# Layer-norm arithmetic moved from GpSimd to VectorE in a convolution-attention-recurrence kernel, with extra TensorE products in the last part

## The chip, the cores and the metric

One core of a Trainium2 chip runs the whole program. The metric is the device time of that core in microseconds (us), the median of several executions. TensorE (PE, with PEld for its weight loads), VectorE (DVE), ScalarE (ACT), GpSimd (POOL) and the DMA queue of SyncE (SP) each run their own list of instructions in order and wait for one another through semaphores.

## The reference, cut to what matters

The input x is 4 batches of 64 channels and 1024 positions (tokens).

```python
x = x + wo @ (softmax(k^T q) v)             # "conv": per batch, 1024 x 1024 scores, no scale
t = to_tokens(x)
t = t + causal_attention(ln(t))             # 8 heads of 64, then @ Wo    (ln: layer norm 1)
t = t + ffn(ln(t))                          # (ln: "norm 3")
# ffn: Wx = ln(t) @ W^T, batch norm over all tokens, then
#      y[t] = sigmoid(Wx[t] + y[t-1] @ V^T) over 1024 steps
```

Both layer norms take each token's mean and variance over 64 channels. The recurrence is solved by sweeps over all positions at once and the last step's change is tested against a limit.

## The kernel before

The main part is a loop over 352 **items** in numbered **slots**. An item is one 128 x 512 tile of scores: TensorE makes it in a bank (L511 conv, L537 attention), ScalarE takes exp of it twice (L775 into `probs`, f32; L779 into `probs_high`, f16), GpSimd subtracts the two into `probs_low` (`pool_low`, L1250), and TensorE multiplies high and low parts by the values (L574, L576, L578) six slots later. Every fourth item of conv and every sixth of attention is "whole": it is used in f32 (L570) and has no work for GpSimd. Slots 0 to 63 are conv, a unit of 16 for each batch. From slot 64 a **unit** is a pair of heads of one batch: 18 slots, in nine **pairs** of slots; at each even slot two items are made, and four units make a batch.

Two units ahead of their use, TensorE makes the raw scores of a later unit (L483, L497) in two banks and VectorE takes their row maxima (L903, two for each pair; L897 in conv). The same two banks serve each pair, so TensorE can't write the masks (L483) of a pair before VectorE has read the pair before it. The partial maxima of a unit are joined by two instructions at L909, once a unit, which makes them a mark for the length of a unit. VectorE also scales finished outputs (L979, L983), makes the low parts of values, queries and keys (L959, L964, L968), and GpSimd adds the scaled outputs to the tokens (`pool_add`, L1260).

**Norm 1** has statistics and application. VectorE takes the statistics of each 128-token tile (L1004, L1007), adds epsilon (L1013) and makes a first guess of the reciprocal root (L988), for three groups: batch 0, batch 1, batches 2 and 3 together (`LN1_GROUPS`), at slots 22, 75 and 129 (`LN1_START_SLOT`). GpSimd refines the guess with three Newton steps of four instructions (`pool_newton`, L1271 to L1274), and in `pool_ln1` subtracts the mean (L1286), multiplies (L1288), sets channel 0 to one (L1290) and copies the result beside itself (L1291) into `xh`; this happens at slots 23, 80, 136 and 214, one for each batch. TensorE transposes `xh` at the key slots (L651), ScalarE and VectorE make the high and low keys.

**Norm 3** of batches 0 and 1 (start at slot 237) and of batch 2 (slot 309) goes the same way: VectorE's guess, GpSimd's twelve Newton instructions four slots later, GpSimd's application (`pool_ln3`, L1295, L1296) from 8 slots later. The last batch's norm is done by VectorE with `dve_newton` (L994 to L996, three instructions a step, each linked: the next one starts when a semaphore tells that the one before has finished).

The order on each engine is the order of the program in each slot. On VectorE it is: scaling, maxima, low parts, and last `dve_norms(g)`. So what a norm does at slot g stands behind the maxima of g and ahead of all of the next slot.

**The last part**: TensorE transposes the last norm's output (L584), multiplies by W (L702, L711), VectorE takes the batch statistics (L1144 to L1169), and sweeps follow: TensorE L730, L731 (then L738 to L747), ScalarE L861, L870, L875.

## Time and profile before

| | us |
|---|---|
| median of 3 runs | 570.09 (568.32 to 572.07) |
| the profiled execution: its own time | 568.85 |
| its span, first to last instruction | 567.0 |
| busy: PE / PEld | 490.0 / 323.0 |
| busy: DVE | 398.8 |
| busy: ACT | 429.3 |
| busy: POOL | 424.4 |
| chain that ended last, by engine | PE 45%, DVE 22%, POOL 17%, ACT 9%, issue 6% |

The profiled execution's time is 1.9 us above its span, and 1.2 us below the median. The mean clock that TensorE was granted is 0.974 of full speed. Busy time of PE counts matmuls to their modelled ends, so that a busy PE is not a PE at its peak.

### The profile page before, as it was taken

Reading aid. Unit: us, or ns where it says so; the run is one execution under the profiler, and the core shown is the slowest. Engines: PE = TensorE matmul, PEld = TensorE weight load, DVE = VectorE, ACT = ScalarE, POOL = GpSimd, SP = SyncE. Lnnn points to the kernel's source line nnn. Section 1 sums busy time; section 2 is a strip of 40 time slices with the busy share of each in tenths; the row PEclk is TensorE's granted clock in tenths of the full one; section 3 lists DMA queues with packets and bytes.
Section 4 is the critical chain, followed back from the end, with each engine's and each line's share of the span. In section 5 each row is a group of like instructions: output and inputs, shape, how many; then the busy total and the mean of one; then the engine's idle time right before and its main releaser. Section 6 shows DMA issues by size and latency. Waiting matters only on the chain.

```text
span 567.0 us, 16744 instructions
## 1 busy us (share of the span) xinstructions
PE 490.0 (86%) x6771; PEld 323.0 (57%) x6771; DVE 398.8 (70%) x909; ACT 429.3 (76%) x832; POOL 424.4 (75%) x463
## 2 busy tenths in 40 slices
PE   4699978988799998889999988998999999787783
PEld 1277655655565755565666756565666766564431
DVE  5878888767678786576767676766767786328757
ACT  3488867866778878587888878787888878785593
POOL 3867965857988797968788797899788799985002
PEclk9999999989999999799999999999999999998698
DMA  9100000000000000000000000000000000000001
GB/s 230 68 3 2 2 20 1 4 1 3 1 22 2 3 3 2 3 1 21 2 3 2 4 3 1 21 3 1 1 3 3 2 3 2 2 2 2 0 2 74
DMA packets 3580, 7.46 MB, mean 13 GB/s; under 512 B 1168, under 2 KB 1456, under 8 KB 3376
## 3 DMA queue, kind: packets, MB, share of 16 engines
q1 hardware_dynamic: 3056, 5.34, 3.5%
q8 instruction: 54, 0.88, 0.7%
q10 hardware_dynamic: 448, 1.05, 0.6%
q14 instruction: 22, 0.18, 0.1%
HBM read 4.22 MB, written 1.05 MB: 9 GB/s over the span
## 4 chain that ended last, share of the span: by engine, by line
PE 45%; DVE 22%; POOL 17%; ACT 9%; issue 6%; DMA 1%; DVEq 0%; SPq 0%; POOLq 0%; ACTq 0%
POOL probs_low L1250 10%; PE bank L537 9%; DVE attn_partial_max L903 7%; ACT probs_high L779 6%; PE bank L497 6%; PE bank L570 5%; PE bank L574 4%; DVE conv_partial_max L897 3%; PE bank L578 3%; PE bank L576 3%; PE bank L455 2%; PE bank L522 2%; PE bank L483 2%; PE bank L456 2%; POOL tokens L1260 2%
## 5 line engine op out<-in xcount | busy, mean ns | idle before, releaser
L1250 POOL TENSOR_TENSOR probs_low<-probs,probs_high 128x512 f16<-128x512 f32 x288 | 327.6, 1158 | 77.5 <-ACT probs_high L779 76.7
L775 ACT ACTIVATE probs<-bank 128x512 f32<-128x512 f32 x352 | 214.7, 611 | 84.2 <-PE bank L537 69.0
L903 DVE TENSOR_REDUCE attn_partial_max<-bank 128x1 f32<-128x512 f32 (+2 forms) x288 | 185.3, 685 | 99.5 <-PE bank L497 99.0
L779 ACT ACTIVATE probs_high<-bank 128x512 f16<-128x512 f32 x288 | 176.8, 614 | 0.0
L574 PEld LDWEIGHTS bank<-values_high,probs_high 128*128 128x128 f16 x1152 | 105.7, 98 | 74.2 <-issue 35.8
L574 PE MATMUL bank<-values_high,probs_high 128*128 128x65 f16 x1152 | 128.8, 196 | 15.5 <-POOL probs_low L1250 11.4
L576 PE MATMUL bank<-values_low,probs_high 128*128 128x64 f16 x1152 | 127.6, 194 | 0.0
L578 PE MATMUL bank<-values_high,probs_low 128*128 128x65 f16 x1152 | 127.1, 194 | 0.0
L576 PEld LDWEIGHTS bank<-values_low,probs_high 128*128 128x128 f16 x1152 | 106.9, 99 | 3.2
L578 PEld LDWEIGHTS bank<-values_high,probs_low 128*128 128x128 f16 x1152 | 107.2, 98 | 0.0
L570 PE MATMUL bank<-values,probs 128*128 128x65 f32 x512 | 71.7, 278 | 0.8 <-POOL probs_low L1250 0.8
L570 PEld LDWEIGHTS bank<-values,probs 128*128 128x128 f32 x512 | 64.7, 192 | 3.5 <-POOL probs_low L1250 1.0
L497 PE MATMUL bank<-attn_keys_high,queries_high 64*128 64x512 f16 (+3 forms) x384 | 56.7, 332 | 7.9 <-ACT probs_high L779 6.0
L1260 POOL TENSOR_TENSOR tokens<-scaled_outputs,tokens 128x256 f32<-128x256 f32 x71 | 51.7, 729 | 8.0 <-DVE scaled_outputs L983 3.3
L537 PE MATMUL bank<-queries_high,attn_keys_high 64*128 64x512 f16 (+3 forms) x384 | 55.6, 326 | 1.1 <-ACT probs_high L779 1.1
L537 PE MATMUL bank<-queries_high,attn_keys_low 64*128 64x512 f16 (+3 forms) x384 | 55.5, 325 | 0.0
L537 PE MATMUL bank<-queries_low,attn_keys_high 64*128 64x512 f16 (+3 forms) x384 | 55.5, 325 | 0.0
L897 DVE TENSOR_REDUCE conv_partial_max<-bank 128x1 f32<-128x512 f32 x64 | 42.8, 687 | 5.8 <-PE bank L470 4.7
L983 DVE TENSOR_TENSOR scaled_outputs<-bank,reciprocal_denominators 128x256 f32<-128x256 f32 x72 | 30.6, 425 | 7.6 <-DVE reciprocal_denominators L979 0.5
L522 PE MATMUL bank<-causal_masks,identity_bf 128*128 128x128 bf16 x256 | 27.5, 219 | 6.6 <-ACT probs_high L779 6.4
L497 PEld LDWEIGHTS bank<-attn_keys_high,queries_high 64*128 64x128 f16 x384 | 15.3, 93 | 29.7 <-issue 6.8
L1343 POOL TENSOR_TENSOR x_split<-probs 128x512 f32<-128x512 f32 x4 | 4.2, 1092 | 36.1 <-ACT probs L878 36.1
(192 smaller groups left out, 708.9 us busy)
## 6 DMA issues: line engine op xcount, KB each, us to landing
x_channels<-in_x_cm SPq DMA_DIRECT2D x6, 256.0 KB, 7.6
tokens<-in_x_tm SPq DMA_DIRECT2D x1, 1024.0 KB, 10.4
out<-ln_channels SPq DMA_DIRECT2D x4, 256.0 KB, 2.0
attn_weights<-in_attn_w ACTq DMA_DIRECT2D x1, 512.0 KB, 6.2
attn_keys_split<-attn_keys_high SPq DMA_DIRECT2D x4, 128.0 KB, 2.3
attn_keys_split<-attn_keys_low SPq DMA_DIRECT2D x4, 128.0 KB, 2.4
queries_high<-minus_max_rows SPq DMA_DIRECT2D x32, 2.0 KB
x_channels<-in_x_cm ACTq DMA_DIRECT2D x2, 128.0 KB, 3.2
```

Source lines behind the costliest of these rows:

```text
L497: last[r] = nc.tensor.matmul(prep_bank(m + r)[:, at * P:(at + tiles) * P], q[rows(r), t * P:(t + 1) * P], xs_hi[rows(r), b * N + j0 * P:b ...
L537: last[r] = nc.tensor.matmul(ST[(i + r) % ST_RING][:, at * P:(at + tiles) * P], keys[rows(r), b * N + j * P:b * N + (j + 1) * P], queries[ ...
L570: ins = nc.tensor.matmul(dst, e32[:, item % E_RING, cols], v32[v % 2][:, j, r, :], start=opens, stop=True, skip_group_check=True)
L574: nc.tensor.matmul(dst, hi, v_hi[v % 2][:, j, r, :], start=opens, stop=False, skip_group_check=True)
L576: nc.tensor.matmul(dst[:, 0:C], hi, v_lo[v % 2][:, j, r, :], start=False, stop=False, skip_group_check=True)
L578: ins = nc.tensor.matmul(dst, lo, v_hi[v % 2][:, j, r, :], start=False, stop=True, skip_group_check=True)
L775: ins = nc.scalar.activation(e32[:, i % E_RING, :], o[:], ACT.Exp, scale=scale)
L779: ins = nc.scalar.activation(p_hi[:, i % P_RING, :], o[:], ACT.Exp, scale=scale)
L897: nc.vector.reduce_max(cmx[v % 2][:, t, part:part + 1], o[:], AX).then_inc(s_prep_used, 1)
L903: nc.vector.reduce_max(dst, o[:].rearrange("p (n w) -> p n w", n=n), AX).then_inc(s_prep_used, 1)
L1250: nc.gpsimd.tensor_tensor(out=p_lo[:, i % P_RING, :], in0=e32[:, i % E_RING, :], in1=p_hi[:, i % P_RING, :], op=ALU.subtract).then_inc(s_r ...
L1260: nc.gpsimd.tensor_tensor(out=dst, in0=scaled[:, half % S_RING, :, :], in1=dst, op=ALU.add).then_inc(s_added, 1)
```

## The change

1. **Norm 1's Newton steps and application go to VectorE.** `pool_newton` and `pool_ln1` are gone. `dve_ln1_start` links its guess, and the three slots behind it hold one Newton step each (three linked instructions). `dve_ln1_apply(b, part)` makes two tiles: one `tensor_scalar` for each tile subtracts the mean and multiplies, with its input broadcast over both copies. Four parts make a batch: at slots 26, 27, 28, 29 for batch 0, and at 82, 138 and 212, each with three more at steps of two slots. The last part ends with a linked memset of channel 0.
2. **Norm 3's Newton steps** go to VectorE as well, one for each of the slots 238 to 240 and 310 to 312. GpSimd keeps the application.
3. Key slots of batch 1 move from 88, 92 to 92, 96.
4. **`pe_keep_clock(bank, n)`** puts n products of 128 x 256 bf16 (identity by masks), whose result nobody reads, at five places of the last part: 8, 6, 22, 3 and 18.

```diff
-LN1_APPLY_SLOT = (23, 80, 136, 214)
-KEY_SLOTS = ((32, 34), (88, 92), (154, 160), (226, 232))
+LN1_APPLY_SLOT = (26, 82, 138, 212)
+LN1_APPLY_PACE = (1, 2, 2, 2)
+KEY_SLOTS = ((32, 34), (92, 96), (154, 160), (226, 232))
...
+        def pe_keep_clock(bank, n):
+
+            for _ in range(n):
+                nc.tensor.matmul(bank[:, 0:2 * P], identbf[:], masks[:].rearrange("p a c -> p (a c)"),
+                                 start=True, stop=True)
...
             pe.wait_ge(s_l3t, 2)
+            pe_keep_clock(MX[0], 8)
             pe.wait_ge(s_l3, 3)
             pe_transposes(MX[1], xh3, 2).then_inc(s_tr, 1)
+            pe_keep_clock(MX[0], 6)
             pe.wait_ge(s_trc, 1)
             nc.tensor.matmul(ST[0][:], ffn_w[:, 0, :], xh3T[:, 2 * CW:3 * CW], start=True, stop=True).then_inc(s_wxp, 1)
+            pe_keep_clock(MX[0], 22)
             for t in range(TPC):
                 pe.wait_ge(s_l3, 4 + t)
                 ins = pe_transpose(LN_BANKS[t // 2], xh3, 3, t)
                 if t % 2:
                     ins.then_inc(s_tr, 1)
             pe.wait_ge(s_aux_used, len(AUXES))
+            pe_keep_clock(ST[1], 3)
             for h in range(2):
                 pe.wait_ge(s_trc, h + 2)
...
             pe.wait_ge(s_bn3, 1)
             pe.wait_ge(s_t2c, 2)
+            pe_keep_clock(MX[0], 18)
...
-            rsqrt_start(rstd1[:, cols], var1[:, cols]).then_inc(s_rstd1, 1)
+            dve_rsqrt_start(rstd1[:, cols], var1[:, cols])
+
+        def dve_ln1_apply(b, part):
+
+            if b and part == 0:
+                nc.vector.wait_ge(s_aux, AUX_OF["keys", 2 * b - 1] + 1)
+            for t in (2 * part, 2 * part + 1):
+                n = b * NT + t
+                ins = nc.vector.tensor_scalar(xh[:, t, :, :],
+                                              tok[:, (t * B + b) * C:(t * B + b + 1) * C].unsqueeze(1)
+                                              .to_broadcast([P, 2, C]),
+                                              mv1[:, n, 0:1], rstd1[:, n:n + 1], ALU.subtract, ALU.mult)
+            if part == NT // 2 - 1:
+                link(ins)
+                nc.vector.memset(xh[:, :, :, 0:1], 1.0).then_inc(s_xt, 1)
...
+                if 0 < g - LN1_START_SLOT[group] <= 3:
+                    cols = slice(b0 * NT, b1 * NT)
+                    dve_newton(rstd1[:, cols], var1[:, cols], nwt1[:, cols])
+            for b in range(B):
+                part, odd = divmod(g - LN1_APPLY_SLOT[b], LN1_APPLY_PACE[b])
+                if 0 <= part < NT // 2 and not odd:
+                    dve_ln1_apply(b, part)
...
             for slot, b0, b1 in ((LN3_PAIR_SLOT, 0, 2), (LN3_THIRD_SLOT, 2, 3)):
-                if g == slot:
-                    v, r, _ = ln3_views(b0, b1, 0, NT)
-                    link(nc.vector.tensor_scalar_add(v, mv4[:, :, b0:b1, 1], LN_EPS))
-                    rsqrt_start(r, v).then_inc(s_rstd3, 1)
+                if 0 <= g - slot <= 3:
+                    ln3_rstd(g - slot, b0, b1, ready=s_rstd3)
...
-                for b in range(B):
-                    if g == LN1_APPLY_SLOT[b]:
-                        pool_ln1(b)
                 for n, slot in enumerate((LN3_PAIR_SLOT, LN3_THIRD_SLOT)):
-                    if g == slot + 4:
+                    if g == slot + 8:
                         pool.wait_ge(s_rstd3, n + 1)
-                        v, r, w = ln3_views(2 * n, 2 + n, 0, NT)
-                        pool_newton(r, v, w)
-                    if g == slot + 8:
                         pool.wait_ge(s_added, (B + (2 + n) * H) * NC)
```

## Rows read from the trace of the kernel before

**Rows 1.** Windows, one unit each from L909 to L909: busy us, clock, DMA.

```profile
131.31:158.44 27.13, 23.00 (x347) 15.59 (x348) 18.04 (x36) 20.16 (x40) 23.07 (x34) 1.00 0.01 2
207.56:236.11 28.55, 24.20 (x341) 16.01 (x342) 17.11 (x35) 19.35 (x38) 24.10 (x35) 0.88 0.01 2
236.11:263.34 27.23, 24.46 (x376) 16.71 (x374) 20.23 (x52) 22.11 (x43) 20.56 (x21) 1.00 0.05 12
287.03:310.72 23.69, 22.54 (x358) 15.43 (x354) 16.50 (x33) 19.85 (x40) 19.82 (x20) 1.00 0.01 2
334.42:362.99 28.57, 24.26 (x366) 16.37 (x362) 20.23 (x52) 21.75 (x42) 22.75 (x23) 1.00 0.05 11
387.88:414.64 26.76, 25.16 (x390) 17.38 (x386) 17.82 (x37) 21.69 (x43) 22.88 (x23) 1.00 0.01 2
438.33:462.38 24.05, 22.70 (x358) 15.45 (x353) 19.03 (x49) 19.91 (x40) 19.89 (x20) 1.00 0.01 2
```

**Rows 2.** Waits, stretch 296.6 to 320.3, a unit that no norm touches.

```profile
DVE attn_partial_max L903 <- PE bank L497: 7.1, 8, 2.0
```

**Rows 3.** Timeline of POOL, 218 to 231: start, us, instruction, idle before.

```profile
220.53 0.23 POOL L1271 TENSOR_TENSOR newton_scratch<-ln_rstd,ln_var_eps 128x16 f32<-128x16 f32 x1
...
223.85 0.22 POOL L1274 TENSOR_TENSOR ln_rstd<-newton_scratch,ln_rstd 128x16 f32<-128x16 f32 x1
224.15 1.05 POOL L1286 TENSOR_TENSOR ln_out<-tokens,ln_mean_var 128x512 f32<-128x512 f32 x1
...
227.12 2.27 POOL L1250 TENSOR_TENSOR probs_low<-probs,probs_high 128x512 f16<-128x512 f32 x2
```

**Rows 4.** Waits of PE, stretch 217 to 246.7.

```profile
PE bank L574 <- POOL probs_low L1250: 3.4, 2, 3.1
```

**Rows 5.** Timeline of POOL and of DVE, 510 to 520.

```profile
511.37 6.73 POOL L1250 TENSOR_TENSOR probs_low<-probs,probs_high 128x512 f16<-128x512 f32 x6
...
513.71 1.08 DVE L988 TENSOR_SCALAR ln_rstd<-ln_var_eps 128x4 int32<-128x4 int32 x1
514.82 1.08 DVE L994 TENSOR_TENSOR ln_newton_scratch<-ln_rstd,ln_var_eps 128x4 f32<-128x4 f32 x1
515.93 1.08 DVE L995 SCALAR_TENSOR_TENSOR ln_newton_scratch<-ln_newton_scratch,ln_rstd 128x4 f32<-128x4 f32 x1
...
518.16 0.17 DVE L994 TENSOR_TENSOR ln_newton_scratch<-ln_rstd,ln_var_eps 128x4 f32<-128x4 f32 x1
```

**Rows 6.** Timeline of DVE, PE and POOL around slots 130 to 134.

```profile
208.46 1.27 DVE L903 TENSOR_REDUCE attn_partial_max<-bank 128x1 f32<-128x512 f32 x2
209.88 0.38 PE L483 MATMUL bank<-causal_masks,identity_bf 128*128 128x128 bf16 x4
210.11 2.27 POOL L1250 TENSOR_TENSOR probs_low<-probs,probs_high 128x512 f16<-128x512 f32 x2 [0.49 <-ACT probs_high L779]
210.74 1.29 DVE L903 TENSOR_REDUCE attn_partial_max<-bank 128x4 f32<-128x512 f32 x2 [0.56 <-PE bank L497]
212.54 2.27 POOL L1250 TENSOR_TENSOR probs_low<-probs,probs_high 128x512 f16<-128x512 f32 x2 [0.16 <-ACT probs_high L779]
213.02 0.39 PE L483 MATMUL bank<-causal_masks,identity_bf 128*128 128x128 bf16 x4
```

**Rows 7.** Timeline of DVE, 525.4 to 527.

```profile
525.45 0.98 DVE L1135 TENSOR_SCALAR ln_tokens<-tokens,ln_mean_var,ln_rstd 128x64 f32<-128x64 f32 x4
```

**Rows 8.** Window 52 to 64, in conv, columns as in rows 1.

```profile
52.00:64.00 12.00, 10.78 (x135) 8.08 (x132) 10.45 (x35) 9.72 (x21) 10.17 (x22) 1.00 0.02 4
```

**Rows 9.** Windows in the last part, columns as in rows 1.

```profile
520.50:530.80 10.30, 7.75 (x22) 4.52 (x23) 7.53 (x37) 2.56 (x5) 0.72 (x1) 0.50 0.00 1
534.20:537.60 3.40, 3.14 (x8) 0.82 (x9) 2.60 (x7) 3.40 (x8) 0.00 (x0) 0.50 0.00 0
```

**Rows 10.** Timeline of PE and ACT, the last part.

```profile
522.08 2.07 PE L702 MATMUL bank<-ln_channels,ffn_weights 128*128 128x512 f32 x2 [0.69 <-ACT ln_channels L845]
525.82 1.14 PE L584 MATMUL bank<-constants,ln_tokens 128*128 128x128 f32 x4 [1.67 <-DVE ln_tokens L1135]
527.08 2.04 PE L711 MATMUL bank<-ln_channels,ffn_weights 128*128 128x256 f32 x4
534.46 0.59 PE L730 MATMUL bank<-wx_fp,identity_fp 128*128 128x512 f16 x1 [2.34 <-ACT y_fp L861]
536.53 3.06 ACT L870 ACTIVATE y_fp<-bank 128x512 f16<-128x512 f32 x6
...
555.19 3.60 PE L752 MATMUL bank<-probs,ffn_weights 128*128 128x512 f32 x8
```

26 lines of the change are left out of this document (1 added, 25 removed).

## The prediction, made before the changed kernel was run

> **What bounds the kernel now.** I read the page first: no engine is saturated (PE 490 us busy of 567, POOL 424, DVE 399) and the chain that ended last changes between PE, DVE, POOL and ACT. So I read the windows unit by unit [rows 1]. A unit of attention that no norm touches lasts 23.69 us; in it POOL is busy for 19.8, DVE for 16.5, and the maxima on DVE wait for TensorE for 7.1 us, some 0.8 us for each of nine pairs [rows 2]. The loop runs at the pace of its dependences, and an engine with idle time still has only a small cushion at each place. Units with norm work are longer: 28.55, 28.57, 27.13 and 26.76 us. The clearest case is batch 2's norm: POOL spends 220.53 to 227.12, 6.6 us, on Newton steps and application [rows 3], TensorE waits 3.4 us for `probs_low` behind it [rows 4], and the unit's mean granted clock is 0.88.
>
> DVE's cushion is uneven. Around slot 130 the masks for the next maxima start at 209.88, 0.15 us after DVE finished its maxima (208.46 + 1.27): TensorE was waiting for DVE. A pair later DVE has 0.56 us idle, and TensorE comes 0.99 us after it (210.74 + 1.29 to 213.02) [rows 6]. So VectorE can take 0.56 + 0.99 = 1.55 us more between slots 130 and 132; beyond that TensorE is late, and behind it scores, exp and everything else.
>
> **What leaves POOL.** I take from each long unit what POOL's block explains, against 23.69 [rows 1].
> - Batch 2: 28.55 − 23.69 = 4.9 us. Rows 4 and the lowered clock fit. The bound above is POOL's whole 6.6.
> - Batch 3 (slot 214, application only): 28.57 − 23.69 = 4.9, but the unit 236 to 263 has the same key work and statistics, no norm on POOL, and 27.23, that is 3.5 over. That leaves 1.3; I take 1.4 for rounding against what falls before the mark.
> - Batch 1: 27.13 − 23.69 = 3.4, with part of the keys' cost in it. I take 2.6.
> - Norm 3 of batches 0 and 1: 26.76 − 23.69 = 3.1, most of it transposes and products by W on TensorE, which stay. I take 0.6. The third batch: the unit up to its start has 24.05, 0.4 over; I take 0.5.
> - Batch 0 in conv: 0.6, little, as units there have other limits.
>
> Together 10.6 us. Below, this could be 6 (only what rows 4 show, and a little of the others), above some 15.
>
> **What comes to DVE, Newton steps.** What does a small DVE instruction cost while POOL works? While POOL runs six `probs_low` back to back from 511.37 (6.73 us), each linked instruction of DVE on four columns takes 1.08 us, and 0.17 us at 518.16, after POOL has ended [rows 5]. It waits out one POOL instruction each time. This holds for `tensor_scalar` (L988), `tensor_tensor` (L994) and `scalar_tensor_tensor` (L995). The Trainium skill states the same as a rule (SBUF — State Buffer, "Who interferes with whom"): a DVE instruction with two SBUF inputs, or in a two-port mode, is blocked until a GpSimd instruction that started first has ended. The trace agrees, with 1.08 against 0.17 us. It is a rule that speaks against this change: it makes of 12 instructions of 0.2 us on POOL nine that may take 1.1 us on DVE.
>
> Two of three steps, at slots 130 and 131, fall between two maxima. Six instructions: 6 × 0.2 = 1.2 us if POOL never holds them, 6 × 1.1 = 6.6 if always. By rows 6, POOL pauses before 210.11 and before 212.54. I lay them in: two pass by 210.1, the third ends at 211.3, the fourth at 212.4, the fifth in the pause, the sixth at 213.7. So about 3.9 us from 209.75, and 3.9 − 1.55 = 2.35, say 2.3 us of delay for TensorE. The third step, behind the maxima of 132, meets a POOL that has run dry, since the scores are late: 0.6 us, in the idle time. Slots 76 to 78, 238 to 240 and 310 to 312 have the same place in their units or nearly so. 4 × 2.3 = 9.2 us (bounds: 0, when 1.2 stays under the cushion, and 4 × 5.0 = 20).
>
> **Application.** Four of today's on 64 columns take 0.98 us [rows 7], so a part of two, of 128 columns each, some 0.55 us unhindered. Each reads and writes SBUF as L988 does, which waits in rows 5; I expect the same here, though its broadcast input is not shown anywhere. Both of a part held: 0.55 + 2 × 1.1 = 2.7 us. When DVE sets the pace, POOL has often finished when a part begins, so I take one wait of some 0.65: 1.2 us a part. Against the cushion of 0.8 each part delays by 0.4: 12 parts give 4.9 us for batches 1 to 3 (bounds 0 and 23). The memset is 0.1 and hidden.
>
> **Batch 0.** Conv from 52 to 64: DVE is busy 10.45 of 12.0 us [rows 8], so 1.55 is free; POOL is busy 10.17, of which some 6 are this norm and go away. Newton 9 × 0.45 = 4.0, four parts × 0.7 = 2.8, minus 1.55, and as much again because four banks, not two, let TensorE run ahead: 3.7, I take 3.5 (bounds 0.5 and 9).
>
> **The last part.** The granted clock is 0.50 (1.2 GHz) from 520.5 to 530.8 and from 534.2 to 537.6, after stretches in which TensorE mostly waited [rows 9]. On the path that sets the end stand L584 (1.14 us) and L711 (2.04 for four pieces of 256 columns); L752's eight pieces of 512 columns at full clock take 3.60, some 0.43 each and so 0.22 for 256 [rows 10]. At 2.4 GHz L711 is bound by its two copies and takes about 1.1, a gain of 0.95; L584 gives 0.3 of 1.14, as its tiles come from DVE one by one; the small product before the batch statistics gives 0.2. The first sweep was slow too, but L870 runs back to back from 536.53 (six in 3.06 us), so ScalarE sets the pace and only 0.1 is won. That is 1.55; I take 1.5. The added products: half of a 512-column product of 0.22 is 0.11 us each at full clock. 22 × 0.11 = 2.4 us behind L702 ends before L584's start at 525.82, if L702 is done by 523; the 18 fit in the 2.3 us idle ahead of L730.
> In the Trainium skill (TensorE: Matmul & The Clock Gate, "What's actually happening") activity releases the throttle. The trace agrees as far as it goes: the clock of 0.50 follows TensorE's idle stretches.
>
> Moving the keys of batch 1 by four slots costs nothing: batch 1's first queries are made at slot 104, and between lie only one unit's rows of maxima in SP's queue.
>
> **Sum.** 9.2 + 4.9 + 3.5 − 10.6 − 1.5 = +5.5 us. The profiled execution, 568.85, becomes 574.4; on the median, 570.09, it is 575.6. I say 574.8.
>
> **Rivals.**
> - *The ports rarely meet (faster).* With POOL rid of the 6.6 us blocks, DVE's instructions fall into its pauses: Newton 2.8 us between the maxima, 1.25 us over the cushion four times = 5.0, parts of 0.8 or less = 0, batch 0 1.5. 6.5 − 10.6 − 1.5 = −5.6: 563 us; with Newton's delay gone too, 5.0 less, 558. For it: POOL's pauses in rows 6. Against it: POOL is busy 84% of an untouched unit. It decides in favour of faster when six instructions take under 2.8 us. 27%.
> - *Parts wait twice (slower).* After each `tensor_scalar` POOL's waiting instruction goes first, and the second waits again: 2.3 us a part instead of 1.2, 12 × 1.1 = +13: 588 us. For it: the chain in rows 5 alternates in just that way. Against it: the two of a part aren't linked. 18%.
> - *The products are in the way.* If the clock stays at 0.50 through the 22, they take 22 × 0.21 = 4.7 us, from 524.2 to 528.9, and L584 is 3.1 us late instead of early: +4.6, 579 us. 8%.
> - My forecast: 45%; 2% left for others.
>
> Range 561 to 586: from the faster rival's neighbourhood to just under the doubled parts. The forecast's own range is 569 to 581. About 1% (5.7 us) is what a measurement of this kernel can tell from no change. Faster by over 1% (below 564.4): most of the first rival, 24%. Slower by over 1% (above 575.8): nearly half of the forecast's own spread and the two slower rivals, 38%. Same 38%.
>
> **What would show it.** In the changed trace, L994 to L996 at slots 130, 131 at 1.1 us each and the masks L483 some 2 us later than their place; if instead they take 0.17, the first rival. The unit 207.56 to 236.11 falls from 28.55 to about 28.0 (−4.9, +2.3, +1.6 and +0.4). The parts' `tensor_scalar` at 0.3 against 1.2 us and more tells the second rival. A POOL row of 6.6 us between two `probs_low` must be gone. In the last part the granted clock must be near 1.00 between 523 and 538 and L711 near 1.1 us; if it is 0.50 with 22 products ahead of L584, the third. I am wrong altogether if DVE's delays don't reach TensorE, that is if idle time on DVE before L903 stays as it was and units are still shorter.

## The result, and the profile after

| | before | after |
|---|---|---|
| median | 570.31 (568.32 to 572.07, 4 runs) | 581.82 (581.04 to 583.14, 4 runs) |
| ratio | | 1.0205, 95% interval 1.0165 to 1.0245 |
| profiled execution: own time, span | 568.85, 567.0 | 581.04, 579.2 |
| mean granted clock | 0.974 | 0.977 |
| busy: PE / DVE / ACT / POOL | 490.0 / 398.8 / 429.3 / 424.4 | 495.3 / 436.1 / 429.4 / 401.4 |
| chain that ended last | PE 45%, DVE 22%, POOL 17% | PE 43%, DVE 35%, POOL 6% |

The change made the kernel slower by 11.5 us, 2%. In a second comparison (experiment 9) the same kernel had 582.19 to 586.56 us in four executions; two more, of 591.37 and 602.92 us, ran in a slower state with a lower granted clock and are left out. Over the eight that are left the median is 582.75, and the profiled one is the fastest of them.

POOL lost 23.0 us of busy time and DVE gained 37.3. In the chain DVE rose by 13 points and POOL fell by 11. The main wait of each of the two engines tells the same (kernel after; us in total, times, longest):

```profile
POOL probs_low L1278 <- ACT probs_high L791: 116.1, 119, 4.6
DVE attn_partial_max L915 <- PE bank L504: 77.8, 87, 2.0
```

POOL now waits 116 us for ScalarE (76.7 before), DVE 78 us for TensorE (99.0 before): the cushion moved from DVE to POOL. Each kernel has its own line numbers; in the changed one L490 is the mask product, L504 the scores for maxima, L787 the first exp, L915 the maxima, L1003 to L1005 the Newton step, L1031 the application, L1278 `probs_low`.

Windows as in [rows 1], kernel after, from L921 to L921: the units of batch 1's and batch 2's norm, an untouched one, and that of norm 3's pair.

```profile
135.28:163.57 28.29, 22.76 (x343) 15.36 (x344) 26.04 (x54) 19.75 (x39) 20.22 (x20) 1.00 0.01 2
213.67:242.81 29.14, 23.16 (x353) 15.63 (x353) 26.22 (x54) 20.06 (x39) 20.85 (x22) 1.00 0.01 2
293.43:317.12 23.69, 22.54 (x358) 15.43 (x353) 16.52 (x33) 19.84 (x40) 19.81 (x20) 1.00 0.01 2
371.09:400.44 29.35, 26.20 (x345) 16.88 (x346) 21.12 (x44) 20.26 (x41) 21.70 (x22) 0.88 0.01 2
```

The untouched unit is again 23.69 us. Batch 2's unit, 28.55 before, is 29.14 though its clock rose from 0.88 to 1.00; norm 3's pair of batches, 26.76 before, is 29.35 and its clock fell to 0.88. In the units of norm 1 DVE is now busy for 26 us of 28 or 29.

**The ledger.** A mean over a unit hides which edit cost what. The kernel has 352 items, and each begins with one exp of a full bank on ScalarE (L787, L775 before). I took the 352 start times of both traces and compared the distance from each even slot to the next: a delay "at slot 130" is what the changed kernel needs more from the exp of item 130 to that of item 132. Outside the slots below the two kernels agree to 0.07 us, mostly to 0.02, so most differences can be put to one edit. A "fall" is a stretch in which the granted clock is 0.50 (1.2 GHz) and not 1.00 (2.4 GHz).

| part | forecast | measured, slots |
|---|---|---|
| batch 0 on DVE | +3.5 | +5.8 (24 to 31) |
| Newton, batch 1 | +2.3 | +1.4 (76, 78) |
| Newton, batches 2 and 3 | +2.3 | +1.5 (130, 132) |
| Newton, norm 3 of the pair | +2.3 | +4.5 (240, 242) |
| Newton, norm 3 of the third | +2.3 | +3.5 (312) |
| application of batches 1 / 2 / 3 | 1.6 each | +1.4 / +3.75 / +2.5 (90; 140, 144, 146; 216 to 220) |
| key slots of batch 1 | 0 | +1.0 (94, 96) |
| POOL relieved of batch 1 / 2 / 3 | −2.6 / −4.9 / −1.4 | −1.7 / −4.9 / −0.8 (86, 88; 142; 222) |
| POOL relieved of norm 3, and of batch 0 | −1.1, −0.6 | −2.5 (254, 302, 324, 326), 0 |
| a fall of the clock that before had at 121.2 | 0 | −1.4 (68, 74) |
| start | 0 | −0.4 |
| last part | −1.5 | −1.4 |
| sum | +5.5 | +12.2 |

The spans give the same, 579.2 − 567.0 = 12.2. Where two edits act on the same slots, the ledger has only their sum. Slots 86, 88 and 142 hold the relief of POOL together with parts of the application, which experiment 7 takes apart. And batch 1's keys left slots 88 and 92 for 92 and 96, so some of what slots 86 and 88 gained may be what 94 and 96 lost: no run moves the keys alone. POOL's block of 6.6 us [rows 3] was worth 4.9, as forecast; what took its place on DVE cost more.

**The Newton steps, as predicted, and what is queued behind them.** Timeline of DVE, kernel after, slots 130 to 131, and then of POOL:

```profile
214.68 1.29 DVE L915 TENSOR_REDUCE attn_partial_max<-bank 128x1 f32<-128x512 f32 x2
215.88 0.17 DVE L1003 TENSOR_TENSOR newton_scratch<-ln_rstd,ln_var_eps 128x16 f32<-128x16 f32 x1
216.08 0.17 DVE L1004 SCALAR_TENSOR_TENSOR newton_scratch<-newton_scratch,ln_rstd 128x16 f32<-128x16 f32 x1
216.29 1.11 DVE L1005 SCALAR_TENSOR_TENSOR ln_rstd<-newton_scratch,ln_rstd 128x16 f32<-128x16 f32 x1
217.44 1.08 DVE L1003 TENSOR_TENSOR newton_scratch<-ln_rstd,ln_var_eps 128x16 f32<-128x16 f32 x1
218.56 0.17 DVE L1004 SCALAR_TENSOR_TENSOR newton_scratch<-newton_scratch,ln_rstd 128x16 f32<-128x16 f32 x1
218.76 0.17 DVE L1005 SCALAR_TENSOR_TENSOR ln_rstd<-newton_scratch,ln_rstd 128x16 f32<-128x16 f32 x1
218.97 0.28 DVE L939 TENSOR_SCALAR minus_max_rows<-bank 16x128 f16<-16x128 f32 x1
219.18 1.26 DVE L915 TENSOR_REDUCE attn_partial_max<-bank 128x4 f32<-128x512 f32 x2
```

```profile
216.22 2.27 POOL L1278 TENSOR_TENSOR probs_low<-probs,probs_high 128x512 f16<-128x512 f32 x2 [0.49 <-ACT probs_high L791]
218.78 2.29 POOL L1278 TENSOR_TENSOR probs_low<-probs,probs_high 128x512 f16<-128x512 f32 x2 [0.29 <-ACT probs_high L791]
```

Two instructions pass in POOL's pause at 0.17 us, two wait out one `probs_low` each, and the last two pass again: 3.05 us for six. `minus_max_rows` (L939) and the maxima of the next pair begin only behind them; TensorE waits 0.34 us for the one and 0.66 us for the other.

Norm 3's pair has the same order of work, but it meets POOL otherwise (DVE, then PE; the two instructions before these lines, from 373.11, take 0.34 and 0.17 us):

```profile
373.70 1.14 DVE L1005 SCALAR_TENSOR_TENSOR ln_rstd<-ln_newton_scratch,ln_rstd 128x16 f32<-128x16 f32 x1
374.87 1.08 DVE L1003 TENSOR_TENSOR ln_newton_scratch<-ln_rstd,ln_var_eps 128x16 f32<-128x16 f32 x1
375.98 0.18 DVE L1004 SCALAR_TENSOR_TENSOR ln_newton_scratch<-ln_newton_scratch,ln_rstd 128x16 f32<-128x16 f32 x1
376.19 1.06 DVE L1005 SCALAR_TENSOR_TENSOR ln_rstd<-ln_newton_scratch,ln_rstd 128x16 f32<-128x16 f32 x1
377.29 0.28 DVE L939 TENSOR_SCALAR minus_max_rows<-bank 16x128 f16<-16x128 f32 x1
```

```profile
377.63 0.23 PE L462 MATMUL bank<-value_matrix_high,attn_keys_split 128*128 128x128 f16 x1 [1.37 <-DVE minus_max_rows L939]
...
378.91 0.59 PE L490 MATMUL bank<-causal_masks,identity_bf 128*128 128x128 bf16 x4 [0.63 <-DVE attn_partial_max L915]
```

Here three instructions are held, six take 4.2 us (373.11 to 377.25), and TensorE waits twice: 1.37 us for `minus_max_rows` (L939), which is queued behind the Newton steps here too, and 0.63 us for the maxima. The granted clock then falls to 0.50 at 378.08.

**The application.** All 32 instructions (duration ns, minimum, median and maximum), kernel after:

```profile
L1031 DVE TENSOR_SCALAR ln_out<-tokens,ln_mean_var,ln_rstd x32: 332/398/1237, 61.5 to 344.2; 128x128 f32<-128x128 f32 x32
```

0.33 us when it passes, up to 1.24 when held. The 24 of batches 1 to 3 take 17.3 us together: 14 of them are over 0.5 us, and in three of the twelve parts both are.

### The profile page after: what moved, and what is told of

It is laid out like the page before. It is cut to its first block, busy times and chain, and to the rows that moved or that the text cites. A ratio compares the mean times of both kernels' runs of the same rounds, so it can differ in the third digit from the quotient of the medians.

```text
span 579.2 us, 16871 instructions
## 1 busy us (share of the span) xinstructions
PE 495.3 (86%) x6828; PEld 327.3 (57%) x6828; DVE 436.1 (75%) x990; ACT 429.4 (74%) x832; POOL 401.4 (69%) x387
## 3 DMA queue, kind: packets, MB, share of 16 engines
q10 hardware_dynamic: 448, 1.05, 0.6%
HBM read 4.22 MB, written 1.05 MB: 9 GB/s over the span
## 4 chain that ended last, share of the span: by engine, by line
PE 43%; DVE 35%; ACT 9%; POOL 6%; issue 5%; DMA 1%; DVEq 0%; SPq 0%; POOLq 0%; ACTq 0%
DVE attn_partial_max L915 11%; PE bank L544 9%; ACT probs_high L791 6%; PE bank L504 6%; POOL probs_low L1278 5%; PE bank L577 4%; DVE conv_partial_max L909 4%; PE bank L581 4%; DVE ln_out L1031 3%; PE bank L585 2%; PE bank L529 2%; PE bank L583 2%; PE bank L462 2%; PE bank L490 2%; PE bank L463 2%
## 5 line engine op out<-in xcount | busy, mean ns | idle before, releaser
L1278 POOL TENSOR_TENSOR probs_low<-probs,probs_high 128x512 f16<-128x512 f32 x288 | 328.2, 1157 | 117.0 <-ACT probs_high L791 116.1
L787 ACT ACTIVATE probs<-bank 128x512 f32<-128x512 f32 x352 | 214.9, 612 | 99.8 <-PE bank L544 80.0
L915 DVE TENSOR_REDUCE attn_partial_max<-bank 128x1 f32<-128x512 f32 (+2 forms) x288 | 185.2, 685 | 78.5 <-PE bank L504 77.8
L504 PE MATMUL bank<-attn_keys_high,queries_high 64*128 64x512 f16 (+3 forms) x384 | 56.9, 333 | 9.5 <-ACT probs_high L791 5.9
L909 DVE TENSOR_REDUCE conv_partial_max<-bank 128x1 f32<-128x512 f32 x64 | 42.9, 687 | 5.5 <-PE bank L477 4.7
L490 PE MATMUL bank<-causal_masks,identity_bf 128*128 128x128 bf16 x256 | 27.6, 221 | 8.7 <-DVE attn_partial_max L915 7.7
L529 PE MATMUL bank<-causal_masks,identity_bf 128*128 128x128 bf16 x256 | 28.1, 223 | 6.1 <-ACT probs_high L791 6.0
L504 PEld LDWEIGHTS bank<-attn_keys_high,queries_high 64*128 64x128 f16 x384 | 15.5, 93 | 31.3 <-DVE attn_partial_max L915 10.8
```

The source lines that it names most:

```text
L504: last[r] = nc.tensor.matmul(prep_bank(m + r)[:, at * P:(at + tiles) * P], q[rows(r), t * P:(t + 1) * P], xs_hi[rows(r), b * N + j0 * P:b ...
L787: ins = nc.scalar.activation(e32[:, i % E_RING, :], o[:], ACT.Exp, scale=scale)
L909: nc.vector.reduce_max(cmx[v % 2][:, t, part:part + 1], o[:], AX).then_inc(s_prep_used, 1)
L915: nc.vector.reduce_max(dst, o[:].rearrange("p (n w) -> p n w", n=n), AX).then_inc(s_prep_used, 1)
L1278: nc.gpsimd.tensor_tensor(out=p_lo[:, i % P_RING, :], in0=e32[:, i % E_RING, :], in1=p_hi[:, i % P_RING, :], op=ALU.subtract).then_inc(s_r ...
```

## The experiments

All were compared with the kernel before in runs of the same chip. Experiments 3 to 6 and 12 ran on one chip, 1, 2, 7 and 8 on a second, 9 to 11 on a third, so variants of different groups are compared by their ratios to the kernel before. Where the profiled execution of a variant is read slot by slot, it is by the ledger as above.

**1. The last part alone.** The kernel before with the five groups of products, nothing else:

```diff
+            pe_keep_clock(MX[0], 8)      # and 6, 22, 3, 18 at the same places as in the changed kernel
```

> The kernel before with only the added products of the last part. Both theories of the last part: from the last item's exp to the end the changed trace is 1.4 us shorter. Theory (the products alone did it): 568.9 against 570.3 of the kernel before, and 1.4 us less of span behind the last item. Rival (the last part is shorter as GpSimd or VectorE comes to it in another state): no change, 570.3.

Measured: 568.60 us (566.89 to 571.40, 10 runs) against 569.47 (30 runs): ratio 0.9992, interval 0.9965 to 1.0019. Not to be told from no change, and the interval reaches down to 2 us of gain. The trace shows why it is so little. PE, this variant:

```profile
522.46 1.13 PE L710 MATMUL bank<-ln_channels,ffn_weights 128*128 128x512 f32 x2
533.97 0.38 PE L741 MATMUL bank<-wx_fp,identity_fp 128*128 128x512 f16 x1 [0.42 <-ACT y_fp L872]
554.82 3.93 PE L763 MATMUL bank<-probs,ffn_weights 128*128 128x512 f32 x8
```

The product by W takes 1.13 us, not 2.07 [rows 10], and the first sweep starts 1.3 us sooner behind the last item (17.14 us after item 352 at 516.83; before 534.46 − 516.02 = 18.44). In the changed kernel and in every variant with the products that distance is the same to 0.03 us. But the products stop there, and the clock falls later: from 552.1 in this trace, and the eight f32 products behind the sweeps take 3.93 us instead of 3.60. Part of the gain is given back 20 us behind the edit. The loop is unedited here, and still its trace differs from that of the kernel before by −1.4 us at slots 68 to 74, where the kernel before had a fall of the clock, and by +1.6 us at slots 36 to 40, where this one has it (74.2). So the −1.4 us at slots 68 and 74 in the ledger isn't the change's doing.

**2. Norm 1 back on POOL.** The products and norm 3's Newton steps on DVE stay:

```diff
-LN1_APPLY_SLOT = (26, 82, 138, 212)      # parts on DVE
+LN1_APPLY_SLOT = (23, 80, 136, 214)      # pool_newton and pool_ln1, as before
-KEY_SLOTS = ((32, 34), (92, 96), ...
+KEY_SLOTS = ((32, 34), (88, 92), ...
```

> The changed kernel with all of norm 1 back on GpSimd as before (old slots too); norm 3's Newton steps stay on VectorE and the added products stay. Theory: what is left of the change is +3.4 and +2.0 us by norm 3 and -1.4 by the products, so 570.3 + 4.1 = 574.4. If the two norms' parts add up, this and the run with norm 3 back on GpSimd together explain the whole: 581.8 - 574.4 = 7.4 us for norm 1. Rival (the parts overlap, one hides the other's delay): above 577 or below 572.

Measured: 573.37 us (571.33 to 576.56), ratio 1.0055 (1.0028 to 1.0081), against an expectation of 574.4. So most of the loss belongs to norm 1. Slots 240 and 312 have +3.6 each, with the clock at 0.50 in both, and slots 254 and 302 to 326 have the 2.5 us of POOL's relief: nearly what the changed kernel has there.

**3. Norm 3's Newton steps back on POOL.** Norm 1 stays on DVE:

```diff
-                if 0 <= g - slot <= 3:
-                    ln3_rstd(g - slot, b0, b1, ready=s_rstd3)
+                if g == slot:
+                    ...                                        # guess on DVE
+                    if g == slot + 4:
+                        pool.wait_ge(s_rstd3, n + 1)
+                        ...
+                        pool_newton(r, v, w)
```

> The changed kernel with norm 3's Newton steps back on GpSimd, all else as changed. Theory (port): comparing item starts of the two traces, these steps cost VectorE 4.5 us at slots 242 to 244 and 3.5 us at slot 314, while taking them from GpSimd gave back 1.1 and 1.4 us. So 5.5 us less than the changed kernel: 576.3 against 581.8. Rival (the whole loss is norm 1's, as that is most of what moved): at most 1 us less, 581.

Measured: 580.74 us (578.75 to 581.05), ratio 1.0173 (1.0147 to 1.0200). The time that I expected was missed by 4.4 us, and the intervals of this ratio and of the changed kernel's, 1.0205 (1.0165 to 1.0245), overlap. Yet by slots the edit did what it should: 4.5 us less at 240 and 242, 3.5 less at 312, 1.1 and 1.2 more at 254 and 324 where POOL's blocks are back, 5.6 us net. It was lost elsewhere: +1.6 at slots 90 and 92, +1.4 at 218, 0.6 at 26 to 30, 1.4 in the last part, all places whose code is unchanged, and 0.7 at the start: both spans are 579.2. Windows of two slots from 218 (us, busy by engine, granted clock, DMA), first the changed kernel and then this variant:

```profile
339.88:344.64 4.76, 2.89 (x47) 2.05 (x48) 4.46 (x13) 1.57 (x3) 3.38 (x4) 1.00 0.00 0
```

```profile
342.71:349.17 6.46, 4.78 (x47) 3.22 (x47) 6.02 (x17) 1.58 (x4) 3.40 (x4) 0.60 0.01 3
```

The same 47 matmuls and the same delay before them, but a clock of 0.60 and 1.7 us more (1.4 with the slot behind it). What decides over such a fall was open here; run 9 below takes it up.

**4. Newton steps one to a pair of slots**, so that two never fall between the same maxima:

```diff
-                if 0 < g - LN1_START_SLOT[group] <= 3:
+                wide = (1, 2, 3) if group == 0 else (1, 3, 5)
+                if g - LN1_START_SLOT[group] in wide:
...
-                if 0 <= g - slot <= 3:
-                    ln3_rstd(g - slot, b0, b1, ready=s_rstd3)
+                if g - slot in (0, 1, 3, 5):
+                    ln3_rstd((g - slot + 1) // 2, b0, b1, ready=s_rstd3)
```

> The changed kernel with one Newton step for each pair of slots (behind slots start+1, +3, +5) for the groups in attention, instead of three in a row of slots. Same instructions, same number. Theory (port waits against a small cushion of VectorE between two maxima): three instructions take at most 3.3 us, and mostly 1 to 2.4, against cushions of 1.55, 2.76 and 1.07 us. The four groups' 10.8 us of delay become 3 to 4, so 574 to 575 against 581.8. Rival (VectorE's work in sum is what counts, wherever it stands): no change, 581 to 582.

Measured: 580.60 us (579.82 to 580.77), ratio 1.0179 (1.0158 to 1.0200). By slots the Newton steps of the four groups cost 2.2, 0.8, 0.65 and 1.4 us, 5.0 in all instead of 10.8, so 5.8 of the some 7 us expected were won there. Falls of the clock at 127.1, 164.7 and 246.6, which the changed kernel's trace has not, and a longer last part take 5.1 us of it, and slots 24 to 30, with a longer fall than there, 0.9 us more. A lone step can still cost: at 381.28 two of three instructions are held for 1.0 us each.

**5. Two of three Newton steps with an operand in a bank.** Variance and scratch of the attention groups lie in PSUM, so that no instruction of the step reads two tiles of SBUF:

```diff
+            v, w = in_psum(b0, b1)               # AUX[:, 384:...], AUX[:, 416:...]
+            dve_newton(r, v, w, s_newt if step == 2 else None)
...
+                if g in (78, 132, 240, 312):
+                    pe.wait_ge(s_newt, (78, 132, 240, 312).index(g) + 1)
```

> The changed kernel with variance and scratch of the first two Newton steps of each attention group in a PSUM bank that is free there, so that each instruction reads only one operand from SBUF. Same places, same number of instructions plus one small copy a group; TensorE waits for the second step before it uses the bank again. Theory (the wait is for the SBUF port that VectorE and GpSimd share): each of the six instructions takes 0.2 us with GpSimd busy too, 1.2 us in sum, under the cushion of 1.55; 10.8 us of delay at these groups become 0 to 1.5, so 571 to 572.5 against 581.8. Rival (a linked instruction is slow while GpSimd works for another reason, such as the semaphore): they stay at 1.1 us, 581 to 582.

Measured: 582.38 us (577.50 to 582.99), ratio 1.0191 (1.0139 to 1.0242); 571 to 572.5 was expected. DVE and POOL, at norm 3's pair:

```profile
378.76 0.17 DVE L1008 SCALAR_TENSOR_TENSOR ln_rstd<-bank,ln_rstd 128x16 f32<-128x16 f32 x1
378.97 0.18 DVE L1006 TENSOR_TENSOR bank<-ln_rstd,bank 128x16 f32<-128x16 f32 x1
379.19 0.18 DVE L1007 SCALAR_TENSOR_TENSOR bank<-bank,ln_rstd 128x16 f32<-128x16 f32 x1
379.40 0.17 DVE L1008 SCALAR_TENSOR_TENSOR ln_rstd<-bank,ln_rstd 128x16 f32<-128x16 f32 x1
```

```profile
378.85 2.27 POOL L1308 TENSOR_TENSOR probs_low<-probs,probs_high 128x512 f16<-128x512 f32 x2 [0.22 <-ACT probs_high L794]
```

The mechanism stands: three instructions begin while POOL works and take 0.17 to 0.18 us, and six take 1.2 us instead of 4.2. My edit brought a wait of its own, though. The bank is TensorE's for small products, so TensorE has to wait until the steps have left it:

```profile
379.63 0.28 PE L622 MATMUL bank<-constants,row_max 128*16 128x128 f32 x1 [1.14 <-DVE ln_rstd L1008]
```

The groups cost 1.6, 1.5, 1.1 and 1.3 us, one slot pair earlier than before, 5.5 in all. That would be 5.3 us less than in the changed kernel's trace. And again falls that this trace has not, at 27.5, 164.1 and 345.0, and one more in the last part took the gain.

**6. Products in the stall.** Forty small products ahead of the masks of slots 242 and 314:

```diff
+                if g in (242, 314):
+                    for _ in range(40):
+                        nc.tensor.matmul(OT[1][:, 384:512], identbf[:], masks[:, 0, :], ...)
```

> The changed kernel with 40 products of 128 columns, read by nobody, in TensorE's list ahead of the masks of slots 242 and 314, where it waits for VectorE for some 3 us anyway. Theory (part of the delay there is the clock: it fell to 0.50 at 378.1 for 6.8 us and at 480.5 for 3.4 us): the clock stays at full speed, slot 242 and 244 lose 2.6 instead of 4.5 us and slot 314 2.6 to 2.9 instead of 3.5. In sum 2 to 2.8 us less, 579 to 580 against 581.8. Rival (the clock's fall costs nothing, since the waits are VectorE's): 581 to 583, with 40 x 0.056 = 2.2 us of products in the stall.

Measured: 587.99 us (582.61 to 591.58), ratio 1.0263 (1.0205 to 1.0322): slower than both expectations. PE, this variant:

```profile
383.19 2.40 PE L698 MATMUL bank<-causal_masks,identity_bf 128*128 128x128 bf16 x40
```

The trace has no fall of the clock at slots 240 or 312. But TensorE's longer wait there is the one for `minus_max_rows`, ahead of these products, so they start only behind it and take 2.40 us where 0.63 us were idle: slots 240 and 312 have +3.8 and +4.9 over the kernel before, where the changed kernel has 4.5 and 3.5 with a fall in each. So the edit itself cost 0.7 us; the rest of the 7.1 us between the two spans is a later start, 1.5 us, and falls elsewhere (slots 69, 147 and the last part). The experiment was badly placed and says nothing on whether filling a stall pays; that filler must stand inside the wait and be shorter than it is argued from this, not shown.

**7. Application with the form that also gives out a sum.** It writes something else than the normalized value; its time alone is read.

```diff
                                               mv1[:, n, 0:1], rstd1[:, n:n + 1], ALU.subtract, ALU.mult,
+                                              accum_out=nwt1[:, n:n + 1])
```

> The changed kernel with norm 1's tensor_scalar also writing out a sum for each tile (into scratch, read by nobody), a form that runs at one element a cycle. Theory (the fast form of tensor_scalar reads and writes SBUF through two ports and so waits for GpSimd): the slow form takes its 0.4 us whatever GpSimd does, up to 0.6 with the reading of the sum; none of 32 takes 1.1 us or more. A part takes 0.8 to 1.2 us instead of 0.6 to 2.3. The 8.6 us of delay at batches 1 to 3 become 2 to 5, so 575 to 579 against 581.8. Rival (any SBUF to SBUF instruction of VectorE waits): as slow or slower, 582 to 585.

Measured: 573.37 us (571.41 to 575.49, 10 runs), ratio 1.0066 (1.0043 to 1.0089): better than both expectations. All instructions of the application, this variant:

```profile
L1031 DVE TENSOR_SCALAR_CACHE_REDUCE ln_out<-tokens,ln_mean_var,ln_rstd x32: 385/403/408, 63.1 to 337.9; 128x128 f32<-128x128 f32 x32
L1031 DVE DVE_READ_ACCUMULATOR ln_out<-tokens,ln_mean_var,ln_rstd x32: 71/85/90, 63.4 to 338.3; 128x1 f32 x32
```

The longest of 32 takes 0.408 us where the plain form took up to 1.237, on the same operands, in the same slots, with the same `probs_low` beside it. By slots 7.4 us of delay are gone in batches 1 to 3 (0.75, 0.35, 1.2 at 86 to 90; 0.75, 0.35, 1.1, 0.7 at 140 to 146; 0.4, 1.4, 0.35 at 216 to 220). Against the kernel before, slots 86 and 88 now have −2.8 (−1.7 in the ledger) and slot 142 has −5.3 (−4.9); 1.7 us in sum are left at 90, 146, 218 and 220. The Trainium skill (SBUF — State Buffer, "Who interferes with whom") says that `tensor_scalar` can take both SBUF ports and then excludes GpSimd, but not in the form that also writes out its accumulator. The two traces agree, with 0.408 us at most in the one form and 1.237 in the other.

**8. Everything on POOL, in pieces**, with the products and the key slots of the changed kernel: a Newton step in each of three slots, the application in halves of the tiles.

```diff
-            pool_newton(rstd1[:, group], ...)                  # twelve instructions, then four
+                for group, slots in enumerate(((23, 24, 25), (76, 78, 80), (130, 132, 134))):
+                    if g in slots:
+                        pool_newton_step(...)                  # four instructions
+                    for part in range(2):
+                        if g == LN1_APPLY_SLOT[b] + part * (2 if b == 0 else 4):
+                            pool_ln1(b, part)
```

> The kernel before with GpSimd keeping both norms but in pieces: one Newton step (four instructions, 1.2 us) at a slot, one in each pair of slots in attention, starting right behind the guess; norm 1's application in two halves (about 1.8 us each) two or four slots apart; key slots of batch 1 at 92 and 96; and the added products. Theory (probs_low is finished 3.6 us ahead of its use, so that pieces under that cost nothing, and only the blocks of 6.6 and 2.9 us did): the 10.9 us that the changed kernel gained from GpSimd's relief come without VectorE's delays, 570.3 - 10.9 - 1.4 = 558, or up to 561 as each half of the application costs more than half. Rival (GpSimd's time in sum is what counts, with 84% busy): no gain but the products', 569.

Measured: 568.17 us (566.27 to 571.84, 10 runs), ratio 0.9978 (0.9952 to 1.0004). No 10 us. Batch 2's block at slot 142 is gone (−5.3), but the pieces come back as +1.05 at 130, +0.15 at 144 and +2.2 at 148 and 150, batch 3's as −0.9 and +1.4, and batch 0's in conv as +3.0, with a fall of the clock at 70.5 in it, where one block cost nothing. Batch 1 has −2.9 at 86 and 88 and +0.6 at 90, and +1.0 at the new key slots. So cutting wins at batches 1 and 2 and loses elsewhere; my reading, not shown apart, is that POOL's time in an attention unit is short however it is cut, and only what a block did beyond its length can be won.

**9. The changed kernel once more**, without an edit.

> The changed kernel once more, nothing edited, for a second profiled execution of it and more executions. Theory (falls come by moment): the delays at each slot are the same to some hundredths of a us as in the first profile, but the granted clock falls to 0.50 behind other delays than those at slots 28, 241 and 313, as it did in the three variants whose profiles showed falls at slots 26, 91 and 219 where this kernel's first profile, with the same delays, showed none; each such fall is worth 1.1 to 1.6 us, so single executions differ by one to three of them; median 581 to 583 us. Rival (falls belong to the delays): the clock falls behind the same slots 28, 241 and 313 again, and the item starts agree with the first profile throughout.

Measured: 584.51 us (582.19 to 586.56, 4 runs), ratio 1.0271 (1.0238 to 1.0304). The profiled execution has 586.56 against 581.04 of the first. Windows from the exp of slot 240 to that of 242, and from 218 to 220: in the first trace

```profile
374.91:381.78 6.87, 4.88 (x54) 3.50 (x54) 5.47 (x12) 3.15 (x7) 3.27 (x3) 0.73 0.00 1
```

and here

```profile
381.34:386.96 5.62, 3.59 (x55) 2.84 (x55) 4.84 (x11) 3.15 (x6) 3.26 (x3) 1.00 0.00 1
345.00:351.44 6.44, 4.77 (x46) 3.22 (x47) 6.00 (x17) 1.57 (x3) 3.38 (x4) 0.59 0.01 3
```

One kernel, the same instructions and the same delays at the other slots to 0.02 us (slot 312, with a fall in both, to 0.13); but this execution has no fall at 240 and 242 (2.1 us less for both), and one at 218 (1.4 more, with the slot behind it), one at slots 0 to 6 and one at slot 36 (1.7 each), 0.6 more at 26 to 30. The eight f32 products of the end began in a stretch at 0.50:

```profile
571.57 5.24 PE L764 MATMUL bank<-probs,ffn_weights 128*128 128x512 f32 x8
```

5.24 us where they took 3.60 in the first trace. So a delay alone does not decide: the same one is followed by a fall or not, from execution to execution. Yet in all traces the falls of the loop stand at few places (slots 3, 25 to 28, 31, 36, 69, 91, 143 or 147, 219, 241 and 313). Most are worth 1.1 to 2.1 us; the one of experiment 6 at slot 219 is worth 0.1. This explains what the profiles of experiments 3 to 5 gave back: they were set against the fastest of the changed kernel's eight executions, a draw with few falls. It explains their medians only in part. Against the mean of the changed kernel's two ratios, 1.0238, they are 3.7, 3.4 and 2.7 us lower, where their slots without falls had promised 5.6, 5.8 and 5.3; the other 1.9 to 2.6 us of each stay open.

**10. Experiments 3 and 7 together.**

```diff
+                                              accum_out=nwt1[:, n:n + 1])
...
+                        pool_newton(r, v, w)                   # norm 3, at slot + 4
```

> The changed kernel with two things at once: norm 1 is applied by the instruction that also gives out a sum (which writes something other than the normalized value, its time alone is read), and norm 3's three steps of the first two groups are back on POOL as one block. If the two prices add, it is the kernel with the summing instruction alone, 573.4 us, less the 4.5 and 3.5 us of delay at slots 240 and 312, plus the 1.1 and 1.2 us that a block on POOL costs at slots 254 and 324: 567.7 us, say 567 to 569. If the clock's falls give back most of a removed delay, as the run with norm 3's steps on POOL alone suggested with a median only 1.1 us below the changed kernel's, it is 571.5 to 573.

Measured: 570.15 us (567.71 to 571.94, 12 runs), ratio 1.0024 (1.0003 to 1.0045), between the two expectations. Against experiment 7 it is 0.42% or 2.4 us less. Experiment 7's own trace had 3.6 us at slot 240 and 1.8 at 312 (no fall there) and gave 2.3 back for POOL's blocks: 3.1 net. The prices add, within the intervals, if they are taken from the right trace; my 5.6 had the fall at 312 and the longer one at 240 in it.

**11. Pieces only where they pay.** Experiment 8 with batch 0 and batch 3 as one block each, and the second group's steps two slots later:

```diff
-LN1_APPLY_SLOT = (26, 82, 138, 212)
+LN1_APPLY_SLOT = (23, 82, 138, 214)
-                for group, slots in enumerate(((23, 24, 25), (76, 78, 80), (130, 132, 134))):
+                for group, slots in enumerate(((), (76, 78, 80), (132, 134, 136))):
```

> The kernel before with the products of the last part, and norm 1 on POOL in pieces for batches 1 and 2 only: batch 0 as one block at slot 23 and batch 3's application as one block at slot 214, as before, and the steps of the second group at slots 132, 134 and 136, not 130, 132 and 134. By the slots of the run with everything in pieces (568.2 us): 3.0 us less at slots 30 and 32, half of it a fall of the clock, 1.05 us less at slot 130 and 0.5 us less at slots 220 to 222: 563.6 us if all of it stays, 564 to 566 with what the clock takes back. Rival: the pieces only move delays and falls about, and the time stays at 568 to 569 us, that of the kernel before with the products alone.

Measured: 567.28 us (565.39 to 569.69, 12 runs), ratio 0.9968 (0.9948 to 0.9988). Faster than the kernel before by 2 us, less than expected. The delay at 130 is gone (0.00). Slots 30 and 220 kept +0.8 each.

**12. Whole blocks as before for batches 0 and 3**: four instructions on 512 columns, not eight on 256.

```diff
-                        if g == LN1_APPLY_SLOT[b] + part * spread:
-                            pool_ln1(b, part)
+                    if b in (0, 3):
+                        if g == LN1_APPLY_SLOT[b]:
+                            pool_ln1(b, 0, NT)
```

> The kernel with pieces for batches 1 and 2 (567.28 us, 0.9968 of the kernel before), with the blocks of batches 0 and 3 made of four instructions again, as in the kernel before, not of eight on half the tiles. Theory (POOL's own length is what counts there): slots 30 and 220 lose the 0.77 and 0.80 us that they had over the kernel before, so the ratio falls by 0.0028 to 0.994, 565.7 us if the kernel before has 569.3. Rival: the two delays come from elsewhere, or the clock takes the gain back, and the ratio stays at 0.997.

Measured: 565.31 us (563.52 to 566.88, 7 runs), ratio 0.9938 (0.9912 to 0.9963): 0.6% or 3.5 us faster than the kernel before, and 2.6% faster than the changed one by the two ratios to it (0.9938 / 1.0205). Slots 30 and 220 have −0.03 and −0.02 over the kernel before. One instruction on 512 columns takes 1.05 us and two on 256 take 2 × 0.61 with a gap more.

Its waits of PE, stretch 207 to 240, batch 2's unit:

```profile
PE bank L580 <- POOL probs_low L1261: 3.2, 4, 1.1
```

That is 3.2 us in four waits of at most 1.1, against 3.4 us in two, the longer 3.1 [rows 4]. TensorE waits as long as before, but the granted clock of the stretch is 1.00 where it was 0.88 [rows 1], and the unit is 2.5 us shorter by the ledger (27.0 instead of 29.5). Here pieces seem to win by keeping the clock, not by shortening the wait; in the traces of the other kernels without the block the fall at 227 is gone as well. But that is not all of the gain. By the ledger the batch 1 slots give 1.2 us too (−2.9 at 86 and 88, +0.2 at 76, +0.6 at 90, +1.0 at 94 and 96), and there the clock is 1.00 both before [rows 1] and now. Norm 3's steps in pieces give 0.4 and the last part 0.8.

## Why the prediction was right in its sign and short in its size

575.6 was worked out, 574.8 forecast, 581.8 measured: inside 561 to 586, and slower, but above the forecast's own range of 569 to 581, and the loss of 11.5 us is more than twice the 4.7 forecast. The chance that I gave to slower, 38%, was no more than that of no change, so the sign was barely called. The sums also mix two bases: 574.8 lies between 574.4, on the profiled execution, and 575.6, on the median, for no reason given, and the first rival's 563 is on the profiled execution; on the median it is 564.5, which isn't faster by over 1%. Point by point:

- **Relief of POOL, −10.6: right.** Measured −9.9 by the ledger, and −11.3 if slots 86, 88 and 142 are taken from experiment 7, where the application hardly delays. The step from 28.55 − 23.69 to 4.9 for batch 2 holds (4.9 or 5.3), and so does batch 1's 2.6 (1.7 or 2.8). Batch 3 gave 0.6 less, norm 3 1.4 more, batch 0 nothing. The rival "ports rarely meet" needed this and free steps; the steps were not free.
- **Newton steps, 4 × 2.3 = 9.2: right mechanism, wrong uniformity.** Laid in by POOL's pauses the six were to take 3.9 us and to delay by 3.9 − 1.55. They took 3.05 and delayed by 1.46 at slot 130: the cushion of 1.55 us out of [rows 6] holds to 0.1 us. At 240 they took 4.2 us and delayed by 2.4 without a fall (experiment 9). At 312 they took 4.2 us too, but both traces of the kernel have a fall there. Experiment 7 has none, with 1.8 us at slots 306 to 312, but its six took only 2.9 us. With 2.4 as at 240, an estimate, the sum is 1.4 + 1.5 + 2.4 + 2.4 = 7.7 us, and falls made it 10.8. "Nearly the same place" was the weak half-sentence: three instructions were held at 240 and 312, two at 130, and TensorE's wait for `minus_max_rows` behind them is 1.37 us at 240 and 0.34 at 130.
- **Application, 4.9: mis-sized.** The forecast took 1.2 us for a part and a cushion of 0.8. By the trace 17.3 us over twelve parts are 1.44 a part, and 12 × (1.44 − 0.80) = 7.7, where the ledger has 7.6. That agreement is partly luck: with slots 86, 88 and 142 taken apart by experiment 7, the application cost 9.1 us, 7.4 of which went with the waits. The wait per part was 0.65 in the forecast and is 0.77 or so, as both are held in three parts. So the rival "parts wait twice" happened in 3 of 12. Experiment 7 shows the cause apart from all else: without the wait the twelve parts cost 1.7 us in all.
- **Batch 0, 3.5: the wrong step is the second subtraction.** Newton took 3.5 us by wall time (first step 2.35, the others 0.55 each) and the parts 3.4, together 6.9, near the 6.8 forecast. I took the 1.55 us of free time off twice, "as much again because four banks let TensorE run ahead". Once gives 5.3; measured 5.8, with a short fall in it. In the stretch 55 to 66 TensorE waits 2.5 us for `row_max` (L928) and 2.1 for `value_matrix_low` (L965), against 0.6 and none before (waits of PE, kernel after, then before):

```profile
PE bank L613 <- DVE row_max L928: 2.5, 1, 2.5
PE bank L477 <- DVE value_matrix_low L965: 2.1, 1, 2.1
```

```profile
PE bank L606 <- DVE row_max L916: 0.6, 1, 0.6
```

So what is late next are other instructions of VectorE than the maxima in the four banks. They were on no row that I read.

- **Keys of batch 1, 0: wrong.** Slots 94 and 96 have +0.96 us in each variant with the new key slots, whoever applies the norm, and nothing in experiment 2, which has the old ones. I looked for who waits for the keys, and not for the time that TensorE, ScalarE and DVE need to make them in another pair. Whether the move costs 1.0 us, or slots 88 to 92 give some of it back, is not shown.
- **The last part, −1.5: right in place, partly given back.** The first sweep starts 1.3 us sooner in all traces, L722 (L711 before) takes 1.03 us instead of 2.04 [rows 10], and the rival with the products in the way did not happen: they take 0.11 us each (2.56 for 22). In the first trace 1.4 us are left at the end, in the second none, as the clock falls behind the sweeps.
- **The clock: not in the sum.** I priced it where the kernel before had it low, and nowhere as something that a new delay brings. In the first trace it cost 2.1 us at 240 and 242 and, by the estimate above, 1.0 at 312, and won 1.4 at slot 68; in the second execution falls took 4.4 us more than in the first, and the start 1.2.

By the ledger the errors are −1.5 (Newton without falls), +2.7 (application), +2.3 (batch 0), +1.0 (keys), +0.7 (relief), +0.1 (last part), −0.4 (start) and +1.7 for falls: 6.6, which is the 12.2 measured less the 5.5 forecast, to rounding. The largest are the application and batch 0.

Not settled: the changed kernel's ratio is 1.0205 in one comparison and 1.0271 in the other, whose intervals hardly overlap. Different draws of falls are the likely reason, but over four executions each that is argued and not shown, and another chip is a rival that no run rules out. Nor is it shown what the application would cost in a form that leaves the port alone and writes the right values; I had none.

## What to carry to other kernels

Before work moves from GpSimd to VectorE, look at what else GpSimd does at that time: a VectorE instruction on two SBUF tiles, or a plain `tensor_scalar` from SBUF to SBUF, cost up to 1.1 or 1.2 us here instead of 0.17 or 0.33 when it met a 1.16 us subtraction, and every one delays what is queued behind it. Price it as its held duration less the cushion at that very slot, and read the cushion from the timeline, once for each place. Cutting a long block on an engine with little idle time into pieces is worth a trial, place by place: here it won at batch 2, where the block had been followed by a lower clock, and at batch 1, where it had not, and lost at batches 0 and 3. A variant worth 1% has to be judged over many executions, since one fall more or less is 1 to 2 us.

## What the runs showed of the hardware that was not expected

- The same tile, the same operands: the `tensor_scalar` with a sum takes 0.385 to 0.408 us, never held, and 0.085 us for reading the sum; without it 0.33 free and up to 1.24 held.
- A Newton instruction with one of its inputs in PSUM takes 0.17 to 0.18 us in the midst of GpSimd's 2.27 us, where the same with both in SBUF takes 1.1.
- Two executions of one kernel differ by 5.5 us (581.04 and 586.56): 4.4 us by falls of the clock behind another set of the same delays, 1.2 us by a later start. Elsewhere their instructions keep the same distances to 0.02 us.
- Eight f32 products of 128 x 512 take 3.60 us at full clock and 5.24 when 3.2 us of them lie in a stretch at 0.50.
